# Spreading score rows over the partitions straight from the on-chip buffer, in a two-layer graph kernel

## The reference, cut to what matters

```python
feats = jnp.einsum('bnf,hfu->bhnu', X, W)
e_self = jnp.einsum('bhnu,hu->bhn', feats, a_self)
e_neigh = jnp.einsum('bhnu,hu->bhn', feats, a_neigh)
dense = e_self[..., :, None] + e_neigh[..., None, :]
dense = jax.nn.leaky_relu(dense, negative_slope=0.2)
dense = dense + NEG_BIG * (1.0 - A[:, None, :, :])
att = jax.nn.softmax(dense, axis=-1)
out = jnp.einsum('bhij,bhju->bhiu', att, feats) + b[None, :, None, :]
```

## Time and profile before

| what | us |
|---|---|
| median of 3 runs | 3373.38 (3371.62 to 3376.89) |
| the profiled execution | 3371.02 |
| its span, from the first to the last instruction | 3369.2 |
| TensorE busy in it | 3291.4 |
| VectorE busy | 2387.5 |
| ScalarE busy | 1864.4 |

### The profile page before, as it was taken

The page is one execution under the profiler, slowest core; times in us unless marked ns, Lnnn a source line. Parts: engine busy times, 40 slices in busy tenths (PEclk is TensorE's granted clock), DMA queues, the critical chain, the costliest instruction groups (busy, mean ns, idle before and its releaser), DMA issues.

```text
span 3369.2 us, 125185 instructions
## 1 busy us (share of the span) xinstructions
PE 3291.4 (98%) x57408; PEld 2804.7 (83%) x57408; DVE 2387.5 (71%) x4236; ACT 1864.4 (55%) x2456; POOL 283.6 (8%) x251
## 2 busy tenths in 40 slices
PE   5999999999999999999999999999999999999998
PEld 4978879798896978979789797887979879797896
DVE  4857758587685867858578585785858768586685
ACT  2746547365564645646466473654746547465563
POOL 0020100202001020010201002010020200202001
PEclk8999999999999999999999999999999999999999
DMA  6114141241412315132141421514124141231400
GB/s 189 62 51 135 45 125 54 69 123 40 132 60 83 102 34 141 65 85 94 39 139 54 101 78 43 142 47 123 56 64 127 41 132 60 73 112 34 126 29 25
DMA packets 233486, 280.95 MB, mean 83 GB/s; under 512 B 149888, under 2 KB 149888, under 8 KB 232960
## 3 DMA queue, kind: packets, MB, share of 16 engines
q1 hardware_dynamic: 232960, 272.95, 27.1%
HBM read 205.26 MB, written 34.08 MB: 71 GB/s over the span
## 4 chain that ended last, share of the span: by engine, by line
PE 85%; DVE 7%; DMA 5%; ACT 1%; issue 1%; SPq 0%; DVEq 0%; POOL 0%; ACTq 0%
PE six L856 72%; PE pair L856 10%; DVE mask L695 2%; DMA s_bc<-self_scores 2%; PE six L991 2%; DMA out_dram<-mask 1%; DMA self_scores<-sc_row 1%; PE pair L885 1%; DVE rest L603 1%; PE six L885 1%; DVE x_parts L599 1%; DVE feat L637 1%; ACT step L465 1%; DVE trl L632 0%; ACT trh L430 0%
## 5 line engine op out<-in xcount | busy, mean ns | idle before, releaser
L856 PE MATMUL six<-x_parts,mask 128*128 128x65 bf16 x16384 | 1547.0, 192 | 17.2 <-DVE mask L695 16.6
L856 PEld LDWEIGHTS six<-x_parts,mask 128*128 128x128 fp8e4 x16384 | 1536.2, 97 | 26.0 <-issue 16.0
L856 PE MATMUL six<-rest,mask 128*128 128x65 bf16 x16384 | 1547.1, 195 | 1.5 <-issue 1.2
L856 PE MATMUL six<-third,mask 128*128 128x65 bf16 x16384 | 1546.8, 192 | 0.8 <-issue 0.6
L856 PEld LDWEIGHTS six<-third,mask 128*128 128x128 fp8e4 x16384 | 1536.4, 98 | 1.3 <-issue 1.2
L856 PEld LDWEIGHTS six<-rest,mask 128*128 128x128 fp8e4 x16384 | 1531.0, 96 | 2.5 <-issue 1.8
L465 ACT ACTIVATE step<-s_bc,n_step 128x1024 uint16<-128x1024 f32 x1024 | 1089.4, 1137 | 372.4 <-DVE mask L695 342.9
L695 DVE TENSOR_TENSOR mask<-adj_t,step 128x1024 uint16<-128x1024 uint16 x1024 | 649.9, 685 | 55.9 <-ACT step L465 55.8
L856 PE MATMUL six<-adj_t,x_parts 128*128 128x512 fp8e4 x1536 | 388.4, 380 | 9.1 <-issue 4.9
L408 POOL TENSOR_TENSOR s_bc<-feat,rden 128x512 f32<-128x512 f32 x112 | 124.6, 1117 | 2811.3 <-DVE s_bc L738 2797.6
L856 PEld LDWEIGHTS six<-adj_t,x_parts 128*128 128x128 f16 x1536 | 146.3, 98 | 186.1 <-issue 15.9
(11 more groups left out here) (127 smaller groups left out, 4839.9 us busy)
## 6 DMA issues: line engine op xcount, KB each, us to landing
s_bc<-self_scores SPq DMA_DIRECT2D x128, 512.0 KB, 3.8
mask<-in_adj_dram SPq DMA_DIRECT2D x64, 512.0 KB, 4.0
xs<-in_x_dram SPq DMA_DIRECT2D x128, 256.0 KB, 3.6
adj_nat<-in_adj_dram SPq DMA_DIRECT2D x64, 512.0 KB, 3.5
out_dram<-mask SPq DMA_DIRECT2D x128, 256.0 KB, 3.3
adj_nat<-in_x_dram SPq DMA_DIRECT2D x64, 256.0 KB, 5.7
step<-in_x_dram SPq DMA_DIRECT2D x64, 256.0 KB, 3.8
xs<-in_L_gnn_W_dram SPq DMA_DIRECT2D x1, 2048.0 KB, 11.4
```

What stands on the lines that cost most here:

```text
L856: return pe.matmul(o, l, r, start=start, stop=stop, skip_group_check=True)
```

## The change

The store of the score rows to memory is gone, and with it the memory tensor and its semaphore. `load_scores` reads the row straight from partition h of sc_row, repeated 128 times, and writes it to the 128 partitions of s_bc as before. The heads swap the two buffers, so that even heads use s_bc[1] and odd ones s_bc[0], the one that holds the layer-norm tiles. `first_scores` waits for the two score copies instead of a store; the load of head 1 waits for the last output tile of the old batch. At the turn `first_scores` stands one place earlier in SP's queue, ahead of the output store of tile 7.

```diff
@@ -67,6 +67,8 @@
     XT_BANKS = (6, 7, 6, 7, 0, 1, 0, 1)
     FT_BANKS = (0, 1, 4, 5, 4, 6, 4, 5)
     MAX_BANK = 3
+
+    S_SLOTS = (1, 0)
     TURN_AT = (10, 13, 18, 21)
     FIRST, SECOND = slice(0, HALF), slice(HALF, T)
     CHAIN = 4 + 4 * T
@@ -226,7 +228,6 @@
         qry_ok = signal("qry_ok", 1)
         ones_ok = signal("ones_ok", 1)
         chain = signal("chain", CHAIN)
-        s_stored = signal("s_stored", 2 * 16)
         s_in = [signal(f"s_in{i}", 16 * H // 2) for i in range(2)]
         stepped = signal("stepped", H * T)
         masked = signal("masked", H * T)
@@ -270,8 +271,6 @@
             return v.rearrange("h u -> (h u)").partition_broadcast(P)
 
 
-        s_dram = nc.dram_tensor("self_scores", [H, N], F32, kind="Internal").ap()
-
         def col(c):
             return slice(c * P, (c + 1) * P)
 
@@ -315,21 +314,18 @@
                 sp.wait_ge(y_ok.sem, y_ok.at(b, t + 1))
                 sp.dma_start(out[b, t * P:(t + 1) * P, :], y_out[:, t % 2, :]).then_inc(y_stored[t % 2], 16)
 
-            def store_scores(b, i):
-                sp.wait_ge(sc_f32.sem, sc_f32.at(b, i + 1))
-                half = slice(i * HALF * P, (i + 1) * HALF * P)
-                sp.dma_start(s_dram[:, half], sc_row[0:H, half]).then_inc(s_stored.sem, 16)
-
             def load_scores(b, h):
                 if h >= 2:
                     sp.wait_ge(stepped.sem, stepped.at(b, (h - 1) * T))
-                sp.dma_start(s_bc[:, h % 2], s_dram[h].partition_broadcast(P)).then_inc(s_in[h % 2].sem, 16)
+                sp.dma_start(s_bc[:, S_SLOTS[h % 2]], sc_row[h:h + 1, :].unsqueeze(1).broadcast_to([1, P, N])).then_inc(
+                    s_in[h % 2].sem, 16)
 
             def first_scores(b):
 
-                store_scores(b, 1)
-                sp.wait_ge(s_stored.sem, s_stored.at(b, 32))
+                sp.wait_ge(sc_f32.sem, sc_f32.at(b, 2))
                 load_scores(b, 0)
+                if b >= 1:
+                    sp.wait_ge(y_ok.sem, y_ok.at(b - 1, T))
                 load_scores(b, 1)
 
             for t in range(HALF, T):
@@ -342,13 +338,12 @@
             for s in range(2):
                 sp.wait_ge(xt_ps.sem, xt_ps.at(0, 2 * s + 2))
                 load_adj(0, s)
-            store_scores(0, 0)
             for t in range(T):
                 turn_adj(0, t)
                 if t + 4 < T:
                     load_adj(0, t + 4)
+            first_scores(0)
             for b in range(B - 1):
-                first_scores(b)
                 for s in range(2):
                     sp.wait_ge(deg_row.sem, deg_row.at(b, 5 + s))
                     load_lead(b + 1, 2 * s)
@@ -365,7 +360,6 @@
                 sp.wait_ge(sums_ps.sem, sums_ps.at(b, H * GROUPS))
                 for t in (2, 3):
                     load_adj(b + 1, t)
-                store_scores(b + 1, 0)
                 for t in range(T):
                     if t == 1:
                         sp.wait_ge(agg_ps.sem, agg_ps.at(b, 2 * KC))
@@ -379,8 +373,8 @@
                         store_y(b, t - 2)
                 store_y(b, T - 2)
                 turn_adj(b + 1, T - 1)
+                first_scores(b + 1)
                 store_y(b, T - 1)
-            first_scores(B - 1)
             for h in range(2, H):
                 load_scores(B - 1, h)
             for t in range(T):
@@ -462,7 +456,7 @@
                     if jt == 0:
                         loaded = s_in[h % 2]
                         act.wait_ge(loaded.sem, loaded.at(b, 16 * (h // 2 + 1)))
-                    act.activation(step[:, g % STEP_SLOTS], s_bc[:, h % 2], ACT.Sigmoid, scale=STEP,
+                    act.activation(step[:, g % STEP_SLOTS], s_bc[:, S_SLOTS[h % 2]], ACT.Sigmoid, scale=STEP,
                                    bias=n_step[:, jt, h:h + 1]).then_inc(stepped.sem, 1)
 
                 def weight_exp(o, a, k):
```

## The result

The changed kernel takes 5547.6 us (median of 4 runs, 5536.8 to 5564.7) against 3373.7 for the kernel before (also 4 runs; the table above has three of them). The ratio is 1.6445, with a 95% interval of 1.6402 to 1.6488. The direction was forecast; the size was not: 4738 with a range up to 5250 was said, and 1365 us of loss became 2174. The profiled execution of the changed kernel took 5539.1 us, its span 5537.3.

What follows compares the result with a forecast made beforehand. TensorE was taken to bound the kernel, busy 3291.4 of 3369.2 us. Slow score loads were to lengthen 14 batches by 86.1 us, the first by 75.9, the last by 83.5, together 1365: 4738 us, range 4450 to 5250.

Steps and rivals of the forecast that it cites:

- A load from one partition takes what one engine takes: 20.5 us of moving.: Score loads in the heads: 512 KB out of one partition at 25.6 GB/s, 20.5 us whichever engine moves it.
- The output store lies behind 41 us of score rows, and VectorE waits for it.: Head of a batch: tile 7's output store moves after loads 0 and 1, delaying value parts and first mask, nothing to 41 us.
- the sum: One batch timed from the end of the second score copy: head 7 ends at 195.3 instead of 109.2, 86.1 us longer.
- From load 2 on the queue doesn't run dry, and the heads follow at the pace of the loads.: SP's queue in the heads: 8.4 us of steps are shorter than a load, so loads follow directly; load 7 landed at 178.2.
- the forecast's own signs: Expected in the profile: loads landing over 20 us after issue, steps waiting for the score load in every head, clock dips.
- The half clock, 3 us per batch.: TensorE in the last head: 1.2 GHz for part of it after a pause, 3.0 us added, bounds 0 and 12.
- The rivals.: Other cases: as fast as memory 0.09; two engines' worth, 3632 us, 0.03; half an engine's worth, 7360 us, 0.03.
- The time as fast as memory: Rival: sixteen engines read one partition unhindered, only the turn between batches moves; 3347 to 3380 us, chance 0.09.
- The DMA that doesn't spread: Rival: one engine moves a load's 128 packets in 20.5 us, total as forecast; 0.85 for one or sixteen engines together.

Runs made afterwards that it cites:

- the run with 16 rows: Changed kernel, but each load reads all 16 partitions of the score buffer, each for 8 destinations; 3682 us.
- the run with one engine: Changed kernel with each load cut in two DMAs, 127 partitions and the last one, so that one DMA engine does the work; 4679.8 us.
- the run with 128 own rows: Changed kernel, but each load copies 1024 weight values of each partition to the same partition of the score buffer; 3359.1 us.

## Why the prediction was right and wrong, point by point

- *A load from one partition takes what one engine takes: 20.5 us of moving.* Right. It was read from eight slow packets of a 16 KB store, and the loads land in 21.4 us. That store gave 52 GB/s for eight partitions; that a single one gives half of it was a guess, which the run with 16 rows bears out (7.0 us, as for four engines' worth). Sixteen engines held at 92% moved no more than one engine does, and to the same 128 partitions the same bytes land in 3.3 us when each partition reads its own: the limit is at the source. (At the 27 GB/s of the window shown, 512 KB take 19.4 us, a little less than the 20.5.)
- *The output store lies behind 41 us of score rows, and VectorE waits for it.* Right: 15 waits, 563 us, up to 38.5 each. The first matmul of the batch shown starts at 792.34, 44.7 us after the second score copy; by the sum it is 46.5 (the mask at 45.7 and 0.8 behind it). This is the 530 us of mask waits.
- *From load 2 on the queue doesn't run dry, and the heads follow at the pace of the loads.* Wrong, and this is the step that failed. It counted 8.4 us of steps and 12.0 us of matmuls as work that goes on beside the loads. The matmuls don't: TensorE's program didn't come while a load moved. Masks then stay in use, so steps stop, and the next load, which waits for the steps, isn't issued. Load 2 still came near its time, 49.2 us after the second score copy where 51.2 was said; the queue ran dry ahead of load 4, issued 16 us after load 3 had landed. SP's timeline has the issues of loads 2 and 3, 4, and 5 to 7 (start us, us from the first to the last):

```profile
796.84 12.50 SPq L320 DMA_DIRECT2D s_bc<-sc_row  x2
...
852.98 0.47 SPq L320 DMA_DIRECT2D s_bc<-sc_row  x1
...
878.92 57.77 SPq L320 DMA_DIRECT2D s_bc<-sc_row  x3
```

The last loads should have followed each other every 20.5 us, an adjacency tile between some of them, and follow every 26 to 30, although each of these lands after 20.7. The load issued at 906.60 has landed at 927.3; TensorE starts again at 929.05 and sets masks free, the last two steps that the next load needs run from 932.54 and 935.05, and it is issued at 936.22. One of the forecast's own signs says the same: ScalarE's steps were to wait for the score load in every head, and the list of waits has this 17 times for 128 heads; with one engine it has it 113 times. The sum was about right for a TensorE that has its instructions: in the run with one engine, where they come, the later loads of a batch are issued 20.5 to 21.0 us apart, and it took 4680 us against the 4738 forecast. These are two of its issues:

```profile
750.90 0.66 SPq L322 DMA_DIRECT2D s_bc<-sc_row  x1
...
771.40 0.63 SPq L322 DMA_DIRECT2D s_bc<-sc_row  x1
```

- *The half clock, 3 us per batch.* Mis-sized: the busy time rose by 217 us, 13.6 per batch. Each head follows a stop, and only the last head's was counted. It is a part of the 2167 us above, but not all of it need be lost: with one engine the busy time rose by the same 217, and the total still came out under the forecast.
- *The rivals.* The time as fast as memory (3347 to 3380) is what the run with 128 own rows gives, 3359: that case was worked out well, but its condition, a quick source, doesn't hold for one partition. The DMA that doesn't spread was said to give the forecast's time, and with the load on one engine the time came within 58 us of it. That sixteen engines would give the same time was the error: a load that holds all of them costs some 860 us more than one that holds a single one. None of the rivals gives the measured 5548. What was missing is a rival in which the slow transfer harms work that doesn't need its data.
- *The sign that could have been read before.* Part 3 of the page of the kernel before (packets, MB, share of 16 engines) has a queue that the forecast passed over:

```profile
q8 instruction: 450, 7.37, 0.9%
```

These 450 packets went through the engines that were about to be held for 20 us at a time, and TensorE, the busiest, has by far the most instructions. The Trainium skill, Runtime: NRT & Kernel Launch, section "Instruction fetch mechanics", says that the program comes in blocks of 16 KB by a DMA queue of the sequencer's own, and counts the fetch as mostly hidden. The size agrees with the trace (7.37 MB / 450 = 16.4 KB); that it is hidden holds before the change and not after.

What stays open: at which place an instruction packet waits, in the engine behind reads that hang, or elsewhere, no view here shows. How many engines may be blocked before TensorE starves was tried only for one and for sixteen.

## What to carry to other kernels

A broadcast out of one on-chip partition ran at the rate of one DMA engine, with sixteen engines on it as with one; from memory, or from rows that lie spread over the partitions, the same bytes come several times faster. A transfer that is slow at its source but holds all engines also held back what had to go through them, here the instructions and an output store, for which VectorE waited up to 38.5 us, and a program with hundreds of small matmuls per head needs its own instructions from there: look for the instruction queue's packets in the DMA view, and for idle time of the kind "issue" between matmuls of one tile. If such a transfer can't be avoided, keep it on few engines; here one engine instead of sixteen took some 860 us off, though the kernel before stays far quicker.

## What the runs showed of the hardware that had not been expected

- While all 16 engines held a score load, no instruction packet came in 20 us; before the change, five did. With the load on one engine, five did again. After one packet TensorE ran 128 matmuls with their weight loads. TensorE ran on for some 5 us (in the batch shown load 2 was issued at 796.8, and it stopped at 802.4) and then stood until the load was through.
- One partition gave 25 to 27 GB/s to sixteen engines and to one; by their landings, of which some 1.4 us lie outside the moving, 16 neighbouring partitions gave some 3.6 times as much as one, and 16 partitions 8 apart some 6.7 times (20.0, 5.6 and 3.0 us).
- After stops of 14 us the granted clock was 0.63 (a mixture of the levels 1.2 and 2.4 GHz) in the stop and 0.89 over the 13.3 us of matmuls behind it:

```profile
885.80:900.20 14.40, 0.00 (x0) 0.00 (x0) 6.21 (x8) 5.45 (x6) 0.00 (x0) 0.63 0.78 25
900.30:913.60 13.30, 13.30 (x384) 13.24 (x383) 4.57 (x8) 3.22 (x3) 0.00 (x0) 0.89 0.50 17
```
